# Performer layers: masked copies of the queries instead of the keys, scores over four row groups, token-major keys by transposes

## What is computed

```python
def _favor_phi(x, omega):
    x = x * D_HEAD ** (-0.25)
    u = jnp.einsum('bhsd,dm->bhsm', x, omega)
    nrm = 0.5 * jnp.sum(x * x, axis=-1, keepdims=True)
    phi = jnp.concatenate([jnp.exp(u - nrm), jnp.exp(-u - nrm)], axis=-1)
    return phi * M_FEAT ** (-0.5)
# Qp, Kp = _favor_phi(q, omega[l]), _favor_phi(k, omega[l]); chunks of 128 tokens
kv = jnp.einsum('bhclm,bhcld->bhcmd', Kc, Vc)
kv_pre = jnp.cumsum(kv, axis=2) - kv
scores = jnp.where(mask, jnp.einsum('bhcim,bhcjm->bhcij', Qc, Kc), 0.0)
num = jnp.einsum('bhcij,bhcjd->bhcid', scores, Vc) + jnp.einsum('bhcim,bhcmd->bhcid', Qc, kv_pre)
den = scores.sum(-1) + jnp.einsum('bhcim,bhcm->bhci', Qc, ks_pre)
out = num / (den[..., None] + ATT_EPS)
```

## Time and profile before

| | |
|---|---|
| runs, median | 1721.0 us (1720.63 to 1723.86, 3 runs) |
| the profiled execution, its own time | 1714.54 us |
| its span, first to last instruction | 1712.5 us |
| mean granted TensorE clock | 0.946 of full speed |
| PE, DVE, ACT, POOL busy | 91%, 68%, 54%, 35% |
| chain that ended last | PE 70%, DVE 14%, ACT 8% |

### The profile page before, as it was taken

How to read it: one execution, slowest core, us unless ns; L and a number is a source line. 1 busy time by engine, 2 the same in 40 slices (tenths; PEclk the granted TensorE clock), 3 DMA queues, 4 the chain that set the end, 5 groups by cost and what they waited for, 6 DMA issues and landing times.

```text
span 1712.5 us, 39621 instructions
## 1 busy us (share of the span) xinstructions
PE 1558.5 (91%) x16341; PEld 839.9 (49%) x16341; DVE 1167.4 (68%) x2006; ACT 929.5 (54%) x1626; POOL 592.8 (35%) x552
## 2 busy tenths in 40 slices
PE   7887669999999999789899999999999999999996
PEld 2544335556556565333445354554535445463543
DVE  5786576666556665334877778786877777687873
ACT  2435333534444344245667666766766776676673
POOL 5462000000000000101755556465555656556561
PEclk9999579999999999679999999999999999999998
DMA  7134100000000000201232414233240432324120
GB/s 249 40 114 193 60 0 8 1 22 1 22 21 2 21 2 1 95 1 41 93 116 56 142 43 131 86 89 116 56 150 35 133 106 67 120 64 146 56 80 13
DMA packets 52401, 119.51 MB, mean 70 GB/s; under 512 B 15488, under 2 KB 20352, under 8 KB 50816
## 3 DMA queue, kind: packets, MB, share of 16 engines
q1 hardware_dynamic: 52224, 116.99, 20.9%
HBM read 37.52 MB, written 0.52 MB: 22 GB/s over the span
## 4 chain that ended last, share of the span: by engine, by line
PE 70%; DVE 14%; ACT 8%; issue 4%; POOL 2%; DMA 1%; SPq 0%; DVEq 0%; ACTq 0%; POOLq 0%
PE ps L426 6%; PE ps L436 5%; PE ps L292 5%; PE ps L284 4%; PE ps L274 4%; PE ps L390 4%; PE ps L1602 4%; PE ps L407 3%; PE ps L1655 3%; PE ps L337 3%; PE ps L1664 2%; PE ps L1621 2%; PE ps L2059 2%; PE ps L2061 2%; PE ps L2067 2%
## 5 line engine op out<-in xcount | busy, mean ns | idle before, releaser
L724 POOL TENSOR_TENSOR big<-big 128x512 f32<-128x512 f32 x112 | 145.0, 1295 | 291.7 <-DMA big<-big 291.0
L733 POOL TENSOR_TENSOR big<-big,nm 128x384 f32<-128x384 f32 x224 | 185.3, 849 | 160.1 <-DVE nm L666 160.1
L624 DVE TENSOR_TENSOR big<-ps,big 128x512 f32<-128x512 f32 x224 | 153.5, 685 | 60.5 <-ACT sq L502 40.7
L1446 POOL MEMSET big<- 128x512 f32 x1 | 0.5, 526 | 492.1 <-DVE x L1929 492.1
L557 ACT ACTIVATE big<-big 128x384 f32<-128x384 f32 x224 | 109.4, 522 | 95.3 <-DVE big L676 93.9
L625 DVE TENSOR_TENSOR big<-ps,big 128x512 f32<-128x512 f32 x224 | 152.2, 679 | 0.0
L426 PEld LDWEIGHTS ps<-big 128*64 128x64 f32 x3584 | 120.6, 144 | 52.5 <-ACT big L569 34.2
L725 POOL TENSOR_TENSOR big<-big 128x512 f32<-128x512 f32 x112 | 145.9, 1303 | 0.0
L426 PE MATMUL ps<-big 128*64 128x64 f32 x3584 | 135.3, 231 | 11.0 <-ACT big L569 10.6
L1889 DVE TENSOR_TENSOR big<-ps,fix 128x512 f32<-128x512 f32 x192 | 119.1, 682 | 37.3 <-PE ps L1602 36.9
L673 DVE TENSOR_REDUCE nm<-ps 128x4 f32<-128x384 f32 x224 | 113.2, 547 | 32.8 <-PE ps L390 30.1
(11 more groups left out here) (304 smaller groups left out, 2923.3 us busy)
## 6 DMA issues: line engine op xcount, KB each, us to landing
big<-big SPq DMA_DIRECT2D x224, 256.0 KB, 2.4
big<-big SPq DMA_DIRECT2D x112, 128.0 KB, 2.4
big<-in_F_w SPq DMA_DIRECT2D x18, 512.0 KB, 3.7
big<-in_zero SPq DMA_DIRECT2D x8, 1088.0 KB, 12.5
big<-big SPq DMA_DIRECT2D x84, 64.0 KB, 2.0
big<-in_D_w SPq DMA_DIRECT2D x12, 256.0 KB, 2.9
big<-in_F_wo SPq DMA_DIRECT2D x6, 512.0 KB, 4.2
big<-in_F_w SPq DMA_DIRECT2D x6, 341.0 KB, 3.7
```

What stands on the lines that cost most here:

```text
L624: dve.tensor_tensor(tmp[:, i, w, :], ps[:, k, :], tb[:, 2 * w, :], ALU.mult).then_inc(*part.mark((key, b, p, 0)))
L724: pool.tensor_tensor(Q[:, p, :], tmp[:, i, 0, :], swp[:, i, 0:T], ALU.add).then_inc(*roped.mark((key, b, p)))
L733: pool.tensor_tensor(v, v, nm[:, p % 3, 16 + 4 * h:20 + 4 * h].unsqueeze(2).to_broadcast([128, 4, KW]), ALU.mult)\
```

## The change

The zeroed copies are made of the queries (Qz) instead of the keys; the keys' features are written once (Kf, in two areas of their own), and before the queries' ones, so q and k swap banks and places. The scores run over all four row groups in turn with 256 moving columns, both copies at once. The token-major keys are transposes of Kf, which ACT copies. The scans read Kf alone and stand earlier on DVE, the multiplies stay behind masks. POOL adds the two copies of Qz into Qf. The relu outputs now lie over Qz.

```diff
-        Kz = Area(10740)(B, 4, T)
+        Qz = Area(10740)(B, 4, T)
+        Kf = [Area(9652)(2, T), Area(15604)(2, T)]
...
-        phi_bank = ((3, 0), (1, 2))
+        qk_bank = (1, 0)
+        phi_bank = ((1, 2), (3, 0))
+        q_full = sg("q_full")
...
         def d_kt_pe(pe, l, b):
...
-            for ch in range(3):
-                for g in range(2):
-                    rows = slice(64 * g, 64 * g + 64)
-                    pe.matmul(ps[:, 6 + g, chunk(ch)], dq[rows, b, 1, chunk(ch)], Om[rows, 128 * g:128 * g + 128],
-                              start=True, stop=False, tile_position=(64 * g, 0))
-                for g in range(2):
-                    rows = slice(64 * g, 64 * g + 64)
-                    last = pe.matmul(ps[:, 6 + g, chunk(ch)], dsq[rows, b, 1, chunk(ch)], Bn[rows, 128 * g:128 * g + 128],
-                                     start=False, stop=True, tile_position=(64 * g, 0))
...
+            for g in range(2):
+                pe.wait_ge(*phi.at((l, b, 1, g)))
+                for ch in range(3):
+                    last = pe.transpose(ps[:, 6 + g, chunk(ch)], Kf[b][:, g, chunk(ch)], ident[:, :])
+                last.then_inc(*full[6 + g].mark(("D", l, b, "kt", g)))
...
         def d_scores_pe(pe, l, b, ch):
             if ch == 0:
-                pe.wait_ge(*phi.at((l, b, 1, 1)))
-            for pair in ((0, 1), (2, 3)):
...
+                pe.wait_ge(*phi.at((l, b, 0, 1)))
+            for g in range(2):
+                for r in range(4):
+                    if g == 0 and ch > 0:
                         pe.wait_ge(*masked.at((l, b, ch - 1, r)))
...
+                    rows = slice(32 * r, 32 * r + 32)
+                    last = pe.matmul(ps[:, r, 256 * g:256 * g + 256], Kf[b][rows, g, chunk(ch)], Qz[rows, b, 2 * g:2 * g + 2, chunk(ch)],
+                                     start=True, stop=True, tile_position=(32 * r, 0))
+                    if g == 1:
+                        last.then_inc(*full[r].mark(("D", l, b, ch, r)))
 
         def d_num_pe(pe, l, b, ch):
...
                 pe.wait_ge(*state.at((l, b, ch - 1)))
+                pe.wait_ge(*q_full.at((l, b, 1)))
...
+        def d_kf_act(act, l, b):
             for g in range(2):
...
+                act.activation(Kf[b][:, g, :], ps[:, k, :], ACT.Exp, bias=eps5[:, 2:3]).then_inc(*phi.mark((l, b, 1, g)))
+
+        def d_qz_act(act, l, b, g, odd):
+            k = phi_bank[0][g]
+            if not odd:
                 act.wait_ge(*full[k].at(("D", l, b, "phi", 0, g)))
...
+            ins = act.activation(Qz[:, b, 2 * g + odd, :], ps[:, k, :], ACT.Exp, bias=eps5[:, 4 + odd:5 + odd])
...
-                act.activation(Kt[:, 3 * b:3 * b + 3, 128 * g:128 * g + 128], ps[:, 6 + g, 0:384].rearrange("p (a c) -> p a c", a=3), ACT.Exp,
-                               bias=eps5[:, 2:3]).then_inc(*ktok.mark((l, b, g)))
+                act.activation(Kt[:, 3 * b:3 * b + 3, 128 * g:128 * g + 128], ps[:, 6 + g, 0:384].rearrange("p (a c) -> p a c", a=3),
+                               ACT.Copy).then_inc(*ktok.mark((l, b, g)))
...
             if hd:
-                d_qf_act(act, *hd)
+                d_kf_act(act, *hd)
             if tl:
                 d_rsqrt_act(act, "D1", *tl, 5)
             if hd:
-                d_kz_act(act, *hd, 0)
+                d_qz_act(act, *hd, 0, 0)
...
             if tl:
                 d_h1_act(act, *tl)
             if hd:
-                d_kz_act(act, *hd, 1)
+                d_qz_act(act, *hd, 0, 1)
+                d_qz_act(act, *hd, 1, 0)
+                d_qz_act(act, *hd, 1, 1)
...
+        def d_scan_dve(dve, l, b, g):
+            dve.wait_ge(*phi.at((l, b, 1, 1)))
+            if g == 1:
+                dve.wait_ge(*full[phi_bank[0][1]].at(("D", l, b, "phi", 0, 1)))
+            step(dve, dve_step, dve.tensor_tensor_scan(dsq[:, b, 1 - g, :], Kf[b][:, g, :], Kf[b][:, g, :], 0.0, ALU.add, ALU.max))
+
         def d_sum_dve(dve, l, b, g):
...
+            dve.wait_ge(*q_full.at((l, b, g)))
+            ins = dve.tensor_tensor(dsq[:, b, 1 - g, :], dsq[:, b, 1 - g, :], Qf[:, b, g, :], ALU.mult)
...
                     d_wo_dve(dve, hd[0])
+                d_scan_dve(dve, *hd, 0)
             if tl:
                 d_scale_norm_dve(dve, "D1", *tl)
...
             if hd:
-                d_sum_dve(dve, *hd, 0)
+                d_scan_dve(dve, *hd, 1)
                 d_mask_dve(dve, *hd, 0)
...
+                d_sum_dve(dve, *hd, 0)
                 d_state_dve(dve, *hd)
...
+        def d_pool(pool):
+            for h in range(HALVES):
+                l, b = head_of(h)
+                for g in range(2):
+                    pool.wait_ge(*phi.at((l, b, 0, g)))
+                    pool.tensor_tensor(Qf[:, b, g, :], Qz[:, b, 2 * g, :], Qz[:, b, 2 * g + 1, :], ALU.add).then_inc(*q_full.mark((l, b, g)))
```

More of the change, by code:

```diff
@@ L1485, in build @@
         h1 = dq[:, :, 1, :]
-        rel = Kz
+        rel = Qz
         om_ready, d_q, d_k, d_v, d_sq = sg("om_ready"), sg("d_q"), sg("d_k"), sg("d_v"), sg("d_sq")
@@ L1526, in d_qk_pe @@
             o_wait(pe, l, b)
-            for j in range(2):
-                scored(pe, l, b, j)
-                pe.matmul(ps[:, j, :], Dw[:, j, :], o[:, cols(b)], start=True, stop=True).then_inc(*full[j].mark(("D", l, b, "qk", j)))
+            for j in (1, 0):
+                k = qk_bank[j]
+                scored(pe, l, b, k)
+                pe.matmul(ps[:, k, :], Dw[:, j, :], o[:, cols(b)], start=True, stop=True).then_inc(*full[k].mark(("D", l, b, "qk", j)))
         def d_v_pe(pe, l, b):
@@ L1540, in d_phi_pe @@
             pe.wait_ge(*d_sq.at((l, b, j)))
-            if j == 0:
+            if j == 1:
                 scored(pe, l, b, 3)
@@ L1588, in d_den_pe @@
             for g in range(2):
-                last = pe.matmul(ps[64 * g:64 * g + 64, 5, :], own, dsq[:, b, g, :], start=True, stop=True, tile_position=(0, 64 * g))
+                last = pe.matmul(ps[64 * g:64 * g + 64, 5, :], own, dsq[:, b, 1 - g, :], start=True, stop=True, tile_position=(0, 64 * g))
             last.then_inc(*full[5].mark(("D", l, b, "den")))
@@ L1593, in d_scores_pe @@
             if ch == 0:
-                pe.wait_ge(*phi.at((l, b, 1, 1)))
-            for pair in ((0, 1), (2, 3)):
-                if ch > 0:
-                    for r in pair:
+                pe.wait_ge(*phi.at((l, b, 0, 1)))
+            for g in range(2):
+                for r in range(4):
+                    if g == 0 and ch > 0:
                         pe.wait_ge(*masked.at((l, b, ch - 1, r)))
[L1599 to L1605, removed]
+                    rows = slice(32 * r, 32 * r + 32)
[3 more added lines that the diff above has]
+                        last.then_inc(*full[r].mark(("D", l, b, ch, r)))
         def d_num_pe(pe, l, b, ch):
@@ L1703, in d_pe_half @@
                 d_v_pe(pe, *hd)
-                d_phi_pe(pe, *hd, 0)
+                d_phi_pe(pe, *hd, 1)
             else:
@@ L1709, in d_pe_half @@
             if hd:
-                d_phi_pe(pe, *hd, 1)
+                d_phi_pe(pe, *hd, 0)
                 d_kt_pe(pe, *hd)
@@ L1751, in d_sq_act @@
         def d_sq_act(act, l, b):
-            for j, done in enumerate((d_q, d_k)):
+            for j, done in ((1, d_k), (0, d_q)):
                 act.wait_ge(*done.at((l, b)))
                 act.activation(dsq[:, b, j, :], dq[:, b, j, :], ACT.Square).then_inc(*d_sq.mark((l, b, j)))
-        def d_qf_act(act, l, b):
+        def d_kf_act(act, l, b):
             for g in range(2):
-                k = phi_bank[0][g]
-                act.wait_ge(*full[k].at(("D", l, b, "phi", 0, g)))
[L1760 to L1766, removed]
+                k = phi_bank[1][g]
+                act.wait_ge(*full[k].at(("D", l, b, "phi", 1, g)))
+                act.activation(Kf[b][:, g, :], ps[:, k, :], ACT.Exp, bias=eps5[:, 2:3]).then_inc(*phi.mark((l, b, 1, g)))
+        def d_qz_act(act, l, b, g, odd):
+            k = phi_bank[0][g]
+            if not odd:
+                act.wait_ge(*full[k].at(("D", l, b, "phi", 0, g)))
+            ins = act.activation(Qz[:, b, 2 * g + odd, :], ps[:, k, :], ACT.Exp, bias=eps5[:, 4 + odd:5 + odd])
+            if odd:
+                ins.then_inc(*phi.mark((l, b, 0, g)))
         def d_kt_act(act, l, b):
@@ L1850, in d_qk_dve @@
         def d_qk_dve(dve, l, b):
-            for j, done in enumerate((d_q, d_k)):
-                dve.wait_ge(*full[j].at(("D", l, b, "qk", j)))
-                dve.tensor_scalar(dq[:, b, j, :], ps[:, j, :], DS ** -0.25, Dqk[:, 2 + j:3 + j], ALU.mult, ALU.add).then_inc(*done.mark((l, b)))
+            for j, done in ((1, d_k), (0, d_q)):
+                dve.wait_ge(*full[qk_bank[j]].at(("D", l, b, "qk", j)))
+                dve.tensor_scalar(dq[:, b, j, :], ps[:, qk_bank[j], :], DS ** -0.25, Dqk[:, 2 + j:3 + j], ALU.mult, ALU.add).then_inc(*done.mark((l, b)))
         def d_v_dve(dve, l, b):
@@ L1917, in d_om_dve @@
             if l > 0:
```

(3 more changed lines are left out.)

2 lines of the change are left out of this document (removed).

## The result

The median went from 1720.82 us (four runs) to 1692.32 (four runs, 1688.43 to 1692.69). The ratio is 0.9836, with an interval of 0.9817 to 0.9855: 28.5 us or 1.6% less, where 30.3 us less was forecast (1690.7). In a later series with more runs of both on one chip the changed kernel had 0.9841 of the kernel before (0.9823 to 0.9860). The total is close; the terms under it are not all right, and the profile shows which.

The account below looks back on a forecast made before the run. The order of PE's instructions was taken as the bound. Eleven halves at 2.16 (three chunks) plus 0.59 (h1) gave 30.3 us, from a 1721.0 median to 1690.7; own range 1683 to 1699, reaching 1682 to 1712 with the dip case.

Parts of the forecast that it names:

- The bound: In the Performer, the order of PE's instructions bounds; an edit counts where PE gets shorter and nobody else is late.
- two of the signs named: Profile signs: a chunk of scores 0.9 to 1.0 us on the chain, and a half 32.3 us instead of 35.1.
- the chunk at 0.93 us: One scores chunk on PE: 0.93 us instead of 1.65, saving 0.72, with bounds of 0.86 and 1.72 us.
- the E row: Stage E's score product, four row groups in turn, 4096 columns; its groups start 0.93 us apart, taken as the chunk's price.
- two-at-a-time rival: Row groups run no more than two at a time, so only h1's 6.5 us remains: 1714.5 us, chance 0.08.
- Chunks paid and unpaid: Scores chunks 0, 1 and 2 each shorten PE's chain, 2.16 us a half; chunk 3's 0.72 us becomes PE idle time.
- The cover for the state's mask: DVE's state masking ends 4.8 us after chunk 0's start, the down product comes at 5.06: not held, 0.26 to spare.
- Token-major keys at nothing: Six transposes replace 24 PE instructions, 1.3 us becoming 0.65; counted as nothing because PE waits for h1 behind either.
- h1 at 0.59: On ACT, one exponential instead of two stands ahead of h1, which starts 0.59 us earlier in each half.
- Scans: On DVE, scans move ahead; the norm L1925 just fits, 0 to 0.2 us lost, with h1 having 0.3 slack.
- clock rival: PE idle gaps lower the clock: one dip a half, 1709.4 us, chance 0.12; or it stays low, 1746 us, chance 0.04.
- POOL at nothing: POOL's two full-query adds a half, 1295 ns each, delay nothing; at worst the first mask starts 0.2 us late.

Follow-up runs that it names:

- h1_late: Changed kernel with the second masked exponential put back ahead of h1 on ACT; halves 33.42 and 33.69 us, total 1697.82 us (ratio 0.9891).
- pairs_256: Changed kernel with each scores chunk's row groups in pairs again, still 256 columns; chunk 1.09 us, total 1689.73 us (ratio 0.9844).
- again_3: Changed kernel with chunk 3's four score products of g = 1 done twice; halves 32.85 and 33.12 us, one run of 1692.75 us.
- turned_twice: Changed kernel with each of the six transposes for the token-major keys done twice; halves 32.85 and 33.12 us, total 1695.52 us (ratio 0.9875).
- one_group: Changed kernel with a chunk's row groups one after another, four 256-column instructions each; chunk 1.09 us, one run of 1693.85 us.

## Why the prediction was right, and where it wasn't

**The bound** was read rightly: each edit counted only where PE was on the chain. Steady halves gained 2.30 us, of which 0.57 is h1's place (h1_late) and the rest 3 × 0.57 for three chunks, 2.28 together. Forecast were 0.59 and 3 × 0.72, so two of the signs named failed: a chunk is not 0.9 to 1.0 us and a half not 32.3.

**The term that was mis-sized** is the chunk at 0.93 us, taken from the E row because "shape, type, row groups and column total agree". It measured 1.08. The E row is the distance between two groups that both use four row groups; a chunk here stands between products over all 128 rows. By the single instructions, the rounds are 0.215 apart, but the first takes 0.32 and 0.32 pass from the last to the next product. That is 0.11 at either end, twice a chunk. In E two groups share the two ends: 0.93 and 1.00 (734.49, 735.42, and the next product at 736.42). A cost per group, read inside a run of such groups, holds only a part of the cost of going into its tile shape and out of it. The Trainium skill, "TensorEngine Tiling (Array Packing)", section "Key Properties", says that a change of tiling mode drains TensorE; these ends agree with it. The 3.07 times of the Trainium skill, "TensorE: Matmul & The Clock Gate", section "Measured speedup vs the span model", which I set aside, was nearer than my 3.7: 3.43 over 1.08 is 3.2.

**The reason given for the gain was also incomplete.** I took two at a time as what pairs do and 1.72 as its bound. pairs_256 shows that pairs do as well as four in turn once a group has no more than four instructions in its block. The two-at-a-time rival was priced on the same mistake.

**Chunks paid and unpaid.** Three paid and chunk 3 not, as forecast; again_3 shows it. But the wait ahead of the last numerator is 0.64 and not the 0.8 to 1.3 forecast, because chunk 3, held by chunk 2's masks, takes 1.32 us up to the next product, 0.33 less than before and not 0.72. The cover for the state's mask held. The prediction has 0.26 us for it; its own terms (0.95, 2.49, 0.69, 0.56) add up to 4.69 and not 4.8, and the trace has the mask over 4.94 after chunk 0's start and the down product at 5.35: no wait of the down product for it stands among the waits of 410 to 610 us.

**Token-major keys at nothing**: shown by turned_twice for the eleven halves; its longer total is open. **h1 at 0.59**: shown by h1_late (0.57). **Scans**: L1929 started at 497.84, when the scan and the root were both just over, and h1 kept its slack, as worked out.

**The clock.** Neither clock rival came: 1.00 in the eleven halves, with waits of 0.67 and 0.64 a half, and in turned_twice too. The rule on transposes (the Trainium skill, "TensorE: Matmul & The Clock Gate", section "PE-mode transpose") cost nothing here; nothing in these runs puts it to a harder test.

**POOL at nothing**: right for the two adds of a steady half, which fell where VectorE had no operation with two SBUF operands. (In the first half one add met the scan L1868 and took 1801 ns; the scan kept its 1224.) I took stage F's products as evidence that the engines don't hold each other up, and those read one operand from PSUM.

**The sum.** In the profiles the eleven halves give 25.1 to 25.3 us of a forecast 30.3. The launch gained 28.5 and, in the longer series, 27.0 (1719.81 to 1692.86). The other 2 to 3 us lie outside those halves and I can't place them. The first half, which I counted at 0, took 29.55 us before, and 27.57 and 29.82 in two profiles of the same changed kernel; what follows the Performer scatters by as much. So the forecast came within 1.6 us of the median partly by luck: a term 5 us too large, and 2 to 3 us that no step had.

## What to carry to other kernels

When products on row groups of the array are to run side by side, look at how many instructions one row group gets in a block: interleave them or make them wider. Four in f32, where a matmul is two instructions, cost nothing here, eight cost 0.57 us a chunk, and between them nothing was run. Price such a product with its two ends, where it borders on another tile shape; a row that sits inside a run of its own kind lacks them. And compare a repeated piece of the schedule between profiles, not only the launch: here it resolves a few hundredths of a us where the launch scatters by several us.

## What the runs showed of the hardware

Going past a busy row group: a product for row group 3 began at once with nine instructions waiting ahead of it, three in each of three groups (one_group), but with eight in each of two groups the next groups' first product waited 0.56 us (the kernel before).

Going into a block of products on four row groups and out of it cost about 0.11 us at either end, at a granted clock of 1.00 (0.32 instead of 0.215 for the first and the last round).

VectorE and POOL hold each other up on operations with two SBUF operands: an add of 128x128 on VectorE went from 292 ns to as much as 1344, 1052 more, where a POOL add is about 1300, and a POOL add went from 1295 to 1602 and more. The Trainium skill, "SBUF — State Buffer", section "SBUF: two separate sides", has this as an exclusive lock on a shared pair of ports, which these numbers agree with. Operations with one operand from PSUM kept their time (four masks 2.48 us), as the same page's section "Who interferes with whom" says of a VectorE instruction with at most one SBUF input.
